# Row norms by batch in the second attention layer; raw keys stored by token class in the third

## The reference

```python
# every layer: x = x + _layernorm(layer(_layernorm(x, axis=-1), ...), axis=-1)
def _L1_attn_ref(x, gamma, beta, Wqkv, Wout):        # x is already a normalised copy
    residual = x
    xn = _layer_norm(x, gamma, beta)                 # so rows are normalised twice
    q, k, v = heads(xn @ Wqkv)                       # 16 heads of 8
    q = jax.nn.elu(q) + 1.0
    k = jax.nn.elu(k) + 1.0
    kv = jnp.einsum('bhld,bhle->bhde', k, v)
    qkv_out = jnp.einsum('bhld,bhde->bhle', q, kv)
    denom = jnp.einsum('bhld,bhd->bhl', q, k.sum(axis=2)) + DENOM_EPS
    return residual + merge(qkv_out / denom[..., None]) @ Wout

def _L2_attn_ref(x, w_qkv, w_proj, b_proj, rpe_q_table, rpe_k_table, rpe_v_table):
    # B = 4 batches, N = 512 tokens, H = 16 heads, hd = 8, 63 buckets of relative position
    q, k, v = (qkv[0] * scale, qkv[1], qkv[2])
    attn = jnp.einsum('bhid,bhjd->bhij', q, k)
    rp = _rp_bucket(N)                               # clip(j - i, -31, 31) + 31
    qL = jnp.einsum('bhid,hdm->bhim', q, rpe_k_table)
    attn = attn + jnp.take_along_axis(qL, rp[None, None], axis=-1)
    kL = jnp.einsum('bhjd,hdm->bhjm', k * scale, rpe_q_table)
    attn = attn + jnp.swapaxes(jnp.take_along_axis(kL, rp[None, None], axis=-1), 2, 3)
    attn = jax.nn.softmax(attn, axis=-1)
    out = jnp.einsum('bhij,bhjd->bhid', attn, v)
    ... # plus the value table, summed by bucket
    return x_out @ w_proj.T + b_proj
```

## Time and profile before

| | us |
|---|---|
| median of three runs (2491.42 to 2500.08) | 2492.27 |
| the profiled execution, its own time | 2491.87 |
| its span, first to last instruction | 2489.7 |
| second attention layer, in the span | 1013.6 to 1098.9 |
| third attention layer, preparation | about 1450 to 1524.5 |
| third attention layer, heads on DVE | 1568.7 to about 2018 |

### The profile page before, as it was taken

The page is one execution under the profiler, slowest core; times in us unless marked ns, Lnnn a source line. Parts: engine busy times, 40 slices in busy tenths (PEclk is TensorE's granted clock), DMA queues, the critical chain, the costliest instruction groups (busy, mean ns, idle before and its releaser), DMA issues. The chain is left out here.

```text
span 2489.7 us, 46290 instructions
## 1 busy us (share of the span) xinstructions
PE 1895.2 (76%) x16384; PEld 1300.9 (52%) x16384; DVE 1665.9 (67%) x3998; ACT 1090.1 (44%) x2023; POOL 850.1 (34%) x631
## 2 busy tenths in 40 slices
PE   5888887388777786459999846687878768998656
PEld 2555555155545554247777724444444346887444
DVE  3777776676555565578999952788888875223584
ACT  2666665255544542114444422555555423332442
POOL 3000000675445540113444333444445413950111
PEclk8999999699989988669999966788888768999687
DMA  3011100210000000010000037556566515000000
GB/s 106 29 42 41 36 32 14 69 29 16 16 16 16 16 16 1 5 23 11 21 12 21 11 71 209 148 169 175 170 176 172 144 41 195 26 8 0 6 1 20
DMA packets 127025, 144.96 MB, mean 58 GB/s; under 512 B 73249, under 2 KB 100727, under 8 KB 124046
## 3 DMA queue, kind: packets, MB, share of 16 engines
q1 hardware_dynamic: 126862, 142.80, 20.2%
HBM read 94.48 MB, written 40.81 MB: 54 GB/s over the span
## 5 line engine op out<-in xcount | busy, mean ns | idle before, releaser
L454 ACT ACTIVATE l0a_pr<-l0a_sm,l0a_nm 128x512 f32<-128x512 f32 x256 | 185.1, 724 | 143.6 <-DVE l0a_nm L367 143.1
L367 DVE CUSTOM_DVE_ANT_0 l0a_sm<-l0a_ps_s,l0a_tb 128x512 f32<-128x512 f32 x256 | 170.8, 685 | 88.1 <-PE l0a_ps_s L522 85.2
L2645 ACT ACTIVATE l2a_pr<-l2a_ps_s,l2a_nm 128x512 f32<-128x512 f32 x256 | 174.1, 686 | 124.2 <-DVE l2a_nm L2564 123.2
L530 PE MATMUL l0a_ps_p<-top_c_ident,l0a_pr 128*128 128x128 f32 x1024 | 169.2, 289 | 54.4 <-ACT l0a_pT L462 53.9
L530 PEld LDWEIGHTS l0a_ps_p<-top_c_ident,l0a_pr 128*128 128x128 f32 x1024 | 109.4, 143 | 116.5 <-ACT l0a_pr L454 65.1
L2564 DVE TENSOR_REDUCE l2a_nm<-l2a_ps_s 128x2 f32<-128x1024 f32 x128 | 156.7, 1225 | 4.4
L2571 DVE STREAM_TRANSPOSE l2a_tt<-l2a_pr 128x1024 f32<-128x1024 f32 x128 | 158.0, 1234 | 0.1
L1582 POOL TENSOR_TENSOR l1f_h<-l1f_lm,l1f_sg 128x512 f32<-128x512 f32 x72 | 92.5, 1284 | 183.4 <-DVE l1f_lm L1646 183.4
L1708 ACT ACTIVATE l1f_csb<-l1f_ps_c,l1f_b3e 128x512 f32<-128x512 f32 x128 | 88.1, 688 | 107.8 <-PE l1f_ps_c L1494 107.6
L807 POOL TENSOR_TENSOR l0f_ct<-l0f_raw,l0f_cos_scaled 128x1024 f32<-128x1024 f32 x32 | 76.0, 2374 | 170.8 <-issue 92.8
L1961 ACT ACTIVATE l2f_h<-l2f_ps_h 128x512 f32<-128x512 f32 x128 | 76.6, 599 | 131.7 <-PE l2f_ps_h L1494 125.7
(11 more groups left out here) (523 smaller groups left out, 5124.2 us busy)
## 6 DMA issues: line engine op xcount, KB each, us to landing
l2a_rawk<-l_k SPq DMA_DIRECT2D x16, 1024.0 KB, 13.4
l2a_qb<-l_qband SPq DMA_DIRECT2D x16, 768.0 KB
l2a_sb<-l_pband SPq DMA_DIRECT2D x32, 384.0 KB
l_qband<-l2a_staged SPq DMA_DIRECT2D x14, 768.0 KB, 15.6
l0a_tb<-l_bias SPq DMA_DIRECT2D x16, 448.0 KB
l2a_ks<-l_k SPq DMA_DIRECT2D x16, 384.0 KB
l_pband<-l2a_pr SPq DMA_DIRECT2D x32, 192.0 KB, 8.8
l_pband<-l2a_pr SPq DMA_DIRECT2D x32, 144.0 KB, 2.1
```

Of the source, the lines that this page charges most:

```text
L367: v.tensor_tensor_reduce(sm[j % 4][:, :], ps_s[j % 2][:, :], tb[slot][:, off:off + N][:, ::-1], -1.0, 3e38, ALU.add, ALU.min, nm[:, j % 4: ...
L454: a.activation(pr[j % 4][:, :], sm[j % 4][:, :], ACT.Exp, bias=nm[:, j % 4:j % 4 + 1], scale=-1.0).then_inc(m["p_ready"], 1)
L530: last = pe.transpose(ps_p[j % 2][:, tile(k)], pr[j % 4][:, tile(k)], ident[:, :])
L2645: a.activation(pr[slot][:, 2 * (g % 2) + u, :], ps_s[g % 2][:, u, :], ACT.Exp, bias=nm[:, g % 2, u:u + 1], accum_out=rs[:, n % 2, 2 * (g % ...
```

## The change

In the second attention layer the two norms of 16 tiles become two norms by batch, `norm_x` and `norm_z`, each with two slots. Before the loop DVE does the statistics of batches 0 and 1 (`row_sums`), `z` of batch 0 and its statistics (`rows`), `zn` of batch 0 (`inputs`), and `rows(1)`. The rest goes into the loop.

In the third attention layer `k32` is stored as `[128, 16 classes, 4 batches, 32]`, so that the tokens of a class lie together. ACT writes `base[..., 2, :]` in that order (innermost stride 32 elements, classes reversed), and the small matmul reads it back in token order. `keys(h)` loads for each of the 128 partitions only the 128 tokens of its class, into one of two buffers, and `expand` reads each of them 16 times by a stride of zero, against the same mask.

```diff
 # l1_attn, DVE
-                ln_in.statistics(v, ch, lambda t: xs[:, t, :], n=T)
-                ln_in.normalize(v, ch, lambda t: xs[:, t, :], lambda t: z[:, t, :], n=T)
-                ch.wait()
-                ln_in.statistics(v, ch, lambda t: z[:, t, :], n=T)
...
+                row_sums(0)
+                row_sums(1)
+                rows(0)
+                inputs(0)
+                rows(1)
...
                 for step in range(B + 2):
                     if step < B:
                         features(step, (0, 1))
+                    if step + 1 < B:
+                        inputs(step + 1)
+                    if step + 2 < B:
+                        row_sums(step + 2)
                     if 1 <= step <= B:
                         block_sums(step - 1)
                     if step < B:
                         features(step, (2, 3))
+                    if step + 2 < B:
+                        rows(step + 2)
 # l2_attn
-            "k32": nc.dram_tensor("l2_k32", (P, T * P), F32).ap(),
+            "k32": nc.dram_tensor("l2_k32", (P, HALF, B, N // HALF), F32).ap(),
...
-                    sp.dma_start(k32[:, cols], base[:, b % 2, 2, :]).then_inc(stored[b % 2], 16)
+                    sp.dma_start(k32[:, :, b, :], base[:, b % 2, 2, :].rearrange("p (c g) -> p c g", c=HALF)).then_inc(stored[b % 2], 16)
...
-                    a.activation(base[:, b % 2, 2, :], ps_q[1], ACT.Copy, scale=SCALE).then_inc(m["base_ready"], 1)
+                    a.activation(base[:, b % 2, 2, :].rearrange("p (c g) -> p g c", c=HALF)[:, :, ::-1], ps_q[1].rearrange("p (g c) -> p g c", c=HALF),
+                                 ACT.Copy, scale=SCALE).then_inc(m["base_ready"], 1)
...
-        rawk = s.sb("rawk", [P, T * P])
+        rawk = [s.sb(f"rawk{i}", [P, T * P // HALF]) for i in range(2)]
...
-                    if h:
-                        sp.wait_ge(m["xk_ready"], h)
-                    src = bass.AP(k32.tensor, k32.offset + h * HD * T * P, [[0, HALF], [T * P, HD], [1, T * P]])
-                    sp.dma_start(rawk[:, :], src).then_inc(m["kl"], 16)
+                    if h >= 2:
+                        sp.wait_ge(m["xk_ready"], h - 1)
+                    each = T * P // HALF
+                    src = bass.AP(k32.tensor, k32.offset + h * HD * T * P, [[each, HALF], [T * P, HD], [1, each]])
+                    sp.dma_start(rawk[h % 2][:, :], src).then_inc(keys_loaded[h % 2], 16)
...
-                    g.tensor_tensor(xk[:, GRP:GRP + T * P].rearrange("p (g c) -> p g c", c=HALF), rawk[:, :].rearrange("p (g c) -> p g c", c=HALF),
+                    g.tensor_tensor(xk[:, GRP:GRP + T * P].rearrange("p (g c) -> p g c", c=HALF), rawk[h % 2][:, :].unsqueeze(2).broadcast_to([P, T * P // HALF, HALF]),
                                     own_shift.unsqueeze(1).broadcast_to([P, T * P // HALF, HALF]), ALU.mult).then_inc(m["xk_ready"], 1)
```

More of the change, by code:

```diff
@@ L1172, in l1_attn @@
         yn = s.sb("yn", [P, NT, D])
-        ln_in = LayerNorm(s, c["half"], T, "ln_in")
+        norm_x, norm_z = RowNorm(s, c["half"], "norm_x"), RowNorm(s, c["half"], "norm_z")
         ln = LayerNorm(s, c["half"])
@@ L1198, in _ @@
             def _(g):
-                ln_in.powers(g, 2, n=T)
-                ln.powers(g, B)
+                norm_x.powers(g, 2)
+                norm_z.powers(g, 2)
+                for step in range(B + 1):
+                    if step + 2 < B:
+                        norm_x.powers(g, step + 3, start=step + 2)
+                        norm_z.powers(g, step + 3, start=step + 2)
+                    if step:
+                        ln.powers(g, step, start=step - 1)
             @block.vector
@@ L1205, in _, with row_sums, rows, inputs @@
                 ch.link(v.memset(va[:, :, :, D:D + 1], 1.0))
-                ln_in.statistics(v, ch, lambda t: xs[:, t, :], n=T)
-                ln_in.normalize(v, ch, lambda t: xs[:, t, :], lambda t: z[:, t, :], n=T)
-                ch.wait()
-                ln_in.statistics(v, ch, lambda t: z[:, t, :], n=T)
[L1210 to L1215, removed]
+                def row_sums(b):
+                    norm_x.statistics(v, ch, b, lambda t: xs[:, b * NT + t, :])
+                def rows(b):
+                    norm_x.normalize(v, ch, b, lambda t: xs[:, b * NT + t, :], lambda t: z[:, b * NT + t, :])
+                    ch.wait()
+                    norm_z.statistics(v, ch, b, lambda t: z[:, b * NT + t, :])
+                def inputs(b):
+                    norm_z.normalize(v, ch, b, lambda t: z[:, b * NT + t, :], lambda t: zn[:, b * NT + t, :])
+                    ch.wait()
+                    v.sem_inc(zn_ready, 1)
+                row_sums(0)
[3 more added lines that the diff above has]
+                rows(1)
                 def features(b, pair):
@@ L2129, in l2_attn @@
         head_loaded = [m["hl0"], m["hl1"]]
+        keys_loaded = [m["kl0"], m["kl1"]]
         shifts_loaded = [m["kt0"], m["kt1"]]
@@ L2332, in _ @@
                     pe.wait_ge(m["base_ready"], 4 * b + 4)
-                    pe.matmul(ps_g[2 * HEADS * b:2 * HEADS * (b + 1), :], gw[:, :, :].rearrange("p a h -> p (a h)"), base[:, b % 2, 2, :], start=True, stop=True).then_inc(m["gam_ps"], 1)
+                    pe.matmul(ps_g[2 * HEADS * b:2 * HEADS * (b + 1), :].rearrange("p (g c) -> p g c", c=HALF), gw[:, :, :].rearrange("p a h -> p (a h)"),
+                              base[:, b % 2, 2, :].rearrange("p (c g) -> p g c", c=HALF)[:, :, ::-1], start=True, stop=True).then_inc(m["gam_ps"], 1)
                 for i in range(NB // 4):
```

4 lines of the change are left out of this document (2 added, 2 removed).

## The result

| | median of the runs | lowest to highest | profiled execution | its span |
|---|---|---|---|---|
| before | 2495.8 us | 2491.42 to 2500.08 | 2491.87 us | 2489.7 us |
| after | 2453.48 us | 2450.66 to 2460.78 | 2460.78 us | 2459.0 us |

The changed kernel takes 0.9835 of the time before (95% interval 0.9804 to 0.9866), 42 us less by the medians. The prediction was 2439 with a range from 2421 to 2466: the sign and the range hold, and the time lies nearer to rival A (2456) than to the forecast. The profiled execution of after is the slowest of its four, 7 us over the median; that is looked at under the point-by-point part.

The account below looks back on a forecast made before the run. DVE's waits on late keys, with four DMA engines always busy as a bound beside DVE, were taken to bound the heads. 2491.9 - 50.7 - 1 + 2.5 - 4 = 2438.7, say 2439 us, range 2421 to 2466.

Parts of the forecast that it names:

- rival A: Third attention layer: four engines stay the bound, losing only the keys' 2.6 us a head; 26.3 a head, 2456 us; chance 0.17.
- DVE's floor: Third attention layer, heads 2 to 14: without its waits DVE could run a head in 24.2 us instead of 28.9.
- The steady heads, -50.7: Third attention layer, heads 2 to 14: 28.9 falls to 25.0 us a head over 13 heads; ends -64 and -26.
- Sum 23.4 (22.3 to 25.4): Third attention layer: us a head that four DMA engines need for qb, sb and other traffic, without the keys.
- the 0.8 us: Steady heads: allowance added to DVE's 24.2 us, giving 25.0 a head, because the four engines' bound lies close.
- Rival C: Third attention layer: qb or ks arrive as late as the keys did, leaving two small terms; about 2490 us; chance 0.06.
- B: Third attention layer: DVE's floor is reached at once, 24.2 us a head, -61; 2427 us; chance 0.13.
- The slack that covers `xk`: Steady heads: xk ready 1.2 us before PE needs it, with POOL's instruction at 4.5 us; lateness beyond it lengthens the head.
- rival D: Third attention layer: slower, the stride-zero operand makes POOL's expand much longer; 2528 us at 12 us each; chance 0.04.
- Head 0, the start of the block, head 15: Third attention layer, outside the steady heads: -1 (0 to -2), 0 (0 to -2) and 0 us.
- The preparation, +2.5: Preparation: 128-byte pieces in k32 stores +2.0 us, strided operands of ACT and PE +0.5; range +2 to +11.
- The second layer, -4: Second attention layer: start gains 12.6 us, 12.0 moves into the loop, 3.4 of it hidden in waits; -0.6 to -6.7.

Follow-up runs that it names:

- the loads split: Changed kernel with each skewed load (qb, both sb) issued as four transfers, one per batch: 2422.26 us, 0.9727 of the kernel before.
- the repeated one: The changed kernel run once more, nothing else changed: 2456.69 us, 0.9864 of the kernel before.
- the keys alone: Kernel before with only the key load and the preparation's layout changed, second attention layer as before: 2465.93 us, 0.9881.
- the scores' operands ahead: Changed kernel with four-part qb and sb loads kept unsplit, and the qs and ks loads issued in step 0 ahead of qb: 2489.19 us, 0.9964.
- `qb` on two: Changed kernel with qb issued as two transfers of two batches each (outermost dimension two): 2583.15 us, 1.0342 of the kernel before.

## Why the prediction came out as it did

**What bounds the kernel, and DVE's floor.** Right. DVE's floor of 24.2 a head was read off the waits; four kernels reached 24.2 to 24.3. That a stuck share of 0.25 means four engines and a bound was right too, and proved more important than I made it.

**The steady heads, -50.7.** This is the term that failed: 32.6 measured, 26.4 a head where I said 25.0. The step was the sum of what the four engines carry, "Sum 23.4 (22.3 to 25.4)". I put the other traffic at 6.5 us, its bytes at the full rate of the preparation. What it takes can be read instead of assumed: DMA share times length is the time that the engines were busy, whatever the sizes of the pieces. What follows is an estimate, which takes the rest to lie evenly on all 16. After: 0.48 x 26.4 = 12.7 us of all 16 engines. The skewed loads, 1.57 MB, take four engines 15.1 us at 104 GB/s, 16.9 at 93, which is 3.8 to 4.2 of that. So 8.5 to 8.9 are left for the rest, the rate of small pieces that I had only as an end (8.5), and the four engines are busy 24.0 to 25.4 us of 26.4.

The same sum for the kernel before: 0.60 x 28.9 = 17.3, less 3.8 to 4.2, plus 15.1 to 16.9, is 28.6 to 30.0 of 28.9. They were full before and are full to 91 to 96% after; the earlier trace rows held the number for before when I made the forecast. Less the 2.6 that I had for the keys it gives 26.0 to 27.4, above DVE's 24.2, and the forecast would have stood nearer to rival A. Less what the keys do take, 0.60 x 28.9 - 0.48 x 26.4 = 4.7 us, it gives about the 24.0 to 25.4 of after. The price of bytes in this sum is not fixed, though: with the loads split the same bytes keep the engines busy for 0.63 x 24.3 = 15.3 us instead of 12.7.

Then the 0.8 us that I allowed "because the bound of the four engines lies so close" was 2.2. The four engines do not work evenly: a `qb` load holds them for some eight microseconds in one piece, SP's next issue is blocked meanwhile, and `ks` and the band stores come late by that. How much of 26.4 is the sum and how much the blocked queue no run tells apart; one that issues `qs` and `ks` from another engine's queue, with `qb` unsplit, would. Rival A named the four engines, and its 26.3 is the measured time, but in part by luck: the keys took 4.3 to 4.7 us of them, not 2.6, and the head became only 2.5 shorter. By the estimate above the blocked issue took back the rest. Rival C had the mechanism (a new wait for `ks` takes the place of the old one, at 2.9 us a head) but not its size: it was a part of the gain and not all. B needs the split loads.

**The slack that covers `xk`.** I gave it 1.2 us, with POOL's instruction at its old 4.5. PE's wait for `xk` fell to 0.4 us a head. The instruction itself became shorter, so rival D went the other way; the row stands under the last heading.

**Head 0, the start of the block, head 15.** Predicted -1, 0, 0. From the first maximum of head 0 to that of head 2 it is 49.9 before and 49.0 after, -0.9; from the first band copy to head 0 -0.5; from head 15 to the next layer +0.4. Right.

**The preparation, +2.5.** Measured +2.2 against the profiled kernel before, +2.8 between the median of the nine kernels with the new layout and small pieces (78.0) and that of the four with the old (75.3): right. The pieces, +2.0 in the sum, are 2.1 by the run that undoes them. The strided operands, +0.5, are 0.1 to 0.7. ACT's write became 0.43 us longer (0.61 to 1.04), twice on the path by the prediction's own count; how much of that is hidden the scatter of the preparation, 0.6 us between executions, does not show. The pieces add 1.3 us to the landing of each store, where 1.0 was predicted. The Trainium skill (DMA: Bandwidth & Descriptors, "Specifications") has a read-modify-write below 512 bytes; if it doubled each piece's cost the term would have been about +6, and the runs do not show that.

**The second layer, -4.** Measured -5.65 in the layer itself, between -4 and the end of -6.7, and -4.3 with the 1.3 that the next layer gives back. The start gained 12.8 where 12.6 was worked out (the first `zn` ends at 1021.6 and not at 1034.4). The mis-sized term is the cover: with 12.8 gained and 12.0 moved into the loop, 5 us of the moved work must lie in waits, not 3.4. DVE's waits for projections fell by 4.0; where the last microsecond lies I have not traced.

**The sum.** Against its own profiled execution: -32.6 steady, -0.9 head 0, -0.1 start and end of the block, +2.2, -5.65 are -37.1, and the span fell by 30.7. The missing 6.4 are in code that the change leaves alone. Of these, +1.3 stand in the layer between the two and come with the norms in every kernel that has them, so they are a cost of the change, for which the prediction had nothing. The +4.9 from the feed-forward layer behind the heads to the end are not: that stretch took 439.5 us in this execution, 437.3 in the repeated one, 434.6 in the kernel before and 434.0 with the keys alone. The medians, 42 us apart, are therefore the better measure; the parts give 36, the repeated comparison 35 by its medians, and 53 was forecast. The time lies in the range because its upper end allowed 26.9 us a head, which is not a sign that the 25.0 was well founded. Its lower end, 2421, does not quite come out of the terms that it names, which give about 2422.5; nothing hangs on it.

**What would show it.** The keys land in 9.6 us (3 to 10: right), POOL's wait is 13.6 (under 10: just missed), PE's for `xk` 5.0 (under 8), DVE's for scores 13.1 (under 20), the granted clock of the heads 0.90 (over 0.93: missed; 0.93 with the split), heads 26.4 apart (25: missed), the layer 80.7 us (81). The sign for being wrong that I named, "DVE's waits go to `qb` or `ks`" and "a DMA share that still sits at 0.25", is what the profile of after shows.

## What to carry to other kernels

Where the DMA share sits for microseconds at a simple fraction (0.25, 0.13), look at the outermost dimension of the transfer that is under way, and issue it in pieces whose outermost dimension is large enough for all 16 engines (32 rows here), before its bytes or another transfer's are cut: here a few lines were worth 75 us (2497.2 to 2422.7) and made a layout change that had given about 30 worth nothing. To estimate whether a few engines are a bound, add their own loads' time to the share-times-length of all the rest, rather than bytes divided by a rate. Here the long transfer on few engines also held up the queue that issues the next one, and another order moved the wait and made it worse.

## What the runs showed of the hardware that was not expected

An operand of POOL that is read with a stride of zero is cheaper than one that is read in full: the same multiplication over 2048 elements a partition went from 4.52 to 3.67 us, in all 13 of its executions (minimum, median and maximum in ns; before, then after).

```profile
L2501 POOL TENSOR_TENSOR l2a_xk<-l2a_rawk,l2a_masks x13: 4503/4517/4529, 1620.6 to 1965.7; 128x2048 f32<-128x2048 f32 x13
```

```profile
L2525 POOL TENSOR_TENSOR l2a_xk<-l2a_rawk,l2a_masks x13: 3668/3672/3677, 1614.5 to 1929.5; 128x2048 f32<-128x2048 f32 x13
```

An ACT copy of 128x512 that writes with a stride (32 elements apart, backwards) takes 1.04 us (0.61 in the kernel before, into plain rows), where the copies beside it into plain rows take 0.60 and 0.68:

```profile
1488.95 0.60 ACT L2319 ACTIVATE l2a_q<-l2a_ps_s 128x512 f32<-128x512 f32 x1 [13.08 <-issue]
1489.44 0.68 ACT L2320 ACTIVATE l2p_base<-l2a_ps_s,l2p_rel 128x512 f32<-128x512 f32 x1
1490.58 1.04 ACT L2322 ACTIVATE l2p_base<-l2a_ps_s 128x512 f32<-128x512 f32 x1
```

And an issue that normally takes 0.4 to 0.6 us takes far longer when a transfer on few engines is still under way in front of it. Behind `qb` on four engines, over 13 heads each, it takes 3.9 to 8.2 us in the changed kernel, 2.0 to 7.1 in its repeat and 3.1 to 5.7 with the scores' operands ahead; behind `qb` on two, 4.4 to 7.7 for `sb` and then 7.3 to 10.4 for `qs`. What exactly fills up there, the queue's room for one engine or something else, no run here tells apart.
